# Last stage of a two-layer attention and expert kernel: residual state and its statistics forward in VectorE's chain, attended values ahead of an up block, fourth norm applied by ScalarE

## The chip, the cores and the metric

One core of one Trainium2 chip runs the whole program. Its engines work side by side and meet through semaphores: TensorE (PE in the rows; PEld is its loading of weights), VectorE (DVE), ScalarE (ACT), GpSimd (POOL), and SyncE (SP), which issues plain DMAs. Each engine does its own instructions strictly in order. The metric is device time in microseconds (us) for one launch, lower is better; what is told is the median over repeated runs.

## What is computed

The input x has 32 batches of 256 tokens by 256 features. Four blocks follow each other, each added to x with a gate tanh(g): an attention on a context of 120 tokens, a feed-forward with 8 experts, a second, linear attention, and a second expert block. Only the last two concern the change. Cut to what matters:

```python
# block 3: linear attention, per batch
Q = heads(norm(x2) @ Wq.T + bq); K = heads(ctx @ Wk.T + bk); V = heads(ctx @ Wv.T + bv)
context  = einsum('ld,le->de', softmax(K, over tokens), V)     # per head
attended = Q @ context
x3 = x2 + tanh(g_xattn[1]) * (attended @ Wo.T + bo)
# block 4: experts, h = norm(x3)
scores = sigmoid(h @ Wr); two best of 8; cw = their normalised weights
mlp = sum over 4 experts: cw[e] * ((silu(h @ Wg[e]) * (h @ Wu[e])) @ Wd[e])
out = x3 + tanh(g_ffn[1]) * (mlp + cw[4]*h + cw[6]*h + cw[7]*relu(h) + causal_conv4(h))
```

## The kernel before

The last stage is the function `finish`. It goes over the batches in a software pipeline: `all_steps` calls `step(s, p)` for s from 2 to 36, and inside one step each engine works on several batches at once. Batch s - 2 gets its linear attention, batch s - 3 its fourth norm, routing and first half of gates and ups, batch s - 4 the rest of its experts, batch s - 5 its output; the combination of block 2 and the third norm's statistics for batch s are in VectorE's list as well. The order of every engine's instructions is written out by hand in five functions called `step`, one for each engine. A wait holds up all that stands behind it on the same engine.

The pieces to know, with their lines in the kernel before:

- TensorE: `turn_c` (L2393) turns the context and writes `bank_c`; it waits until VectorE has read the bank in `x3_new`. Then come `down(s-5, 1)` (L2405), which waits for `hidden_low(., 1)`, `values`, `add_rest`, `turn3`, `keys`, an up block, `turn4` (L2445), `queries` (into `bank_x`, waits for `x_turned`), `turn_k`, a gate block, `context`, `logits`, an up block (L80 into `f_ups`), `attended` (into `bank_x`), `output` (into `bank_c`), `down(s-4, 0)` and a gate block.
- VectorE: `own_heads` (L2249, `f_cx`) takes `context` and feeds `attended`. `hidden` (L2158, called twice) makes the product of gates and ups. `route_and_combine` is a chain of small routing instructions in which the two `combine_first` (L1730), the two `combine_second` (L1735), the statistics of the third norm, `hidden_low` (L2212) and `x3_new` (L2330, `f_x`) fill the gaps. After the chain (its last member is L2322) come `weights_turned` (L2143), `stat4` (L2163, L2168), a `silu`, `values_out`, `normalise4` (L2188, `f_x4h`) and `close`.
- ScalarE: `hidden_high` (L2039) follows `hidden`; `x3_own` (L2087, `f_x3p`) follows in its order; `x_turned` (L2045, `f_xT`) empties the turned x3 for `queries`; `attended_out` (L2099) empties `attended` for `output`; `tanh` is L2026.
- GpSimd: `shares` (L1972 to L1978) waits for the whole routing chain; then `keep_x2` (L1947), `norm4` (L1956 to L1961: variance, minus mean, power -1/2, gated share), four gathers by indirect DMA (L1695), `norm3`, and `add_relu` (L1984), which waits for `x3_own`.
- SyncE: `spread_weights` writes the turned weights to DRAM with four DMAs (L1916), waits for them, and reads them back spread over all partitions (L1919, `f_cw_wide`); VectorE's `share_ups` (L2150) wants them in the middle of the next step, before `own_heads`.

## Time and profile before

| | |
|---|---|
| median of 3 runs | 2277.44 us (2277.32 to 2280.03) |
| profiled execution | 2278.87 us, span 2277.1 us |
| granted TensorE clock over the span | 0.993 |
| PE busy | 2174.0 us (95%) |
| DVE busy | 1773.2 us (78%) |
| ACT busy | 1270.6 us (56%) |
| POOL busy | 663.1 us (29%) |

Busy times are sums over the whole span and say which engine has most to do, not which one sets the end of a stage. The last stage begins at 1600 us and takes the remaining 677 us; one of its steps takes a little over 20 us. Times in the rows further down are microseconds from the start of the span; the second number is how long the instruction (or the merged group) ran.

### The profile page before, as it was taken

To read this page: it belongs to the slowest core of one execution; us is meant where nothing else is said; L and a number is where in the kernel's file an instruction comes from. 1 tells how busy PE (TensorE), PEld (TensorE's weight loads), DVE (VectorE), ACT (ScalarE), POOL (GpSimd) and SP (SyncE) were. 2 spreads that over 40 slices of the span, in tenths; PEclk is the share of its full clock that TensorE was granted. 3 is DMA by queue.
4 is the path that set the end of the run, shared out by engine and by line. 5 is a ranking of instruction groups with operands and counts; after the bars stand their busy time and mean duration, and the time that the engine had idled before them with its cause. 6 is when DMAs were issued, how large, how long until landed. Compare 5 with 4: busy or idle time off the path is not lost. (4 is left out here: it accounts for less than half of the span.)

```text
span 2277.1 us, 49508 instructions
## 1 busy us (share of the span) xinstructions
PE 2174.0 (95%) x15998; PEld 1876.2 (82%) x15998; DVE 1773.2 (78%) x6017; ACT 1270.6 (56%) x3251; POOL 663.1 (29%) x1162
## 2 busy tenths in 40 slices
PE   8999999999999999999899999999888889888897
PEld 6777777777777777777799999999688888888886
DVE  5888888888888888888655555555688898888987
ACT  6776677677677667766343333433344444444443
POOL 1123223222322322322200000001555555555541
PEclk9999999999999999999899999999999999999999
DMA  5321011011011011100322222212232222222221
GB/s 185 120 94 30 29 38 39 20 38 39 22 36 38 23 36 38 36 17 28 102 92 84 84 79 80 84 47 71 68 91 86 73 83 91 91 85 73 86 70 47
DMA packets 118302, 146.55 MB, mean 64 GB/s; under 512 B 17458, under 2 KB 100649, under 8 KB 117920
## 3 DMA queue, kind: packets, MB, share of 16 engines
q1 hardware_dynamic: 104905, 121.98, 17.1%
q0 software_dynamic: 12288, 21.21, 3.3%
q8 instruction: 132, 2.16, 0.4%
q14 instruction: 122, 1.00, 0.2%
q10 hardware_dynamic: 855, 0.19, 0.0%
HBM read 101.04 MB, written 54.66 MB: 68 GB/s over the span
## 5 line engine op out<-in xcount | busy, mean ns | idle before, releaser
L711 ACT ACTIVATE a_prob<-a_prob,a_nmax 128x376 f32<-128x376 f32 x512 | 309.8, 606 | 155.5 <-DVE a_nmax L857 155.4
L1457 ACT ACTIVATE e_hidden<-e_first,keep_b 128x256 f32<-128x256 f32 x320 | 134.1, 471 | 283.3 <-PE e_first L80 282.8
L857 DVE CUSTOM_DVE_ANT_0 a_prob<-a_score,a_mask_row 128x376 f32<-128x376 f32 x512 | 266.7, 540 | 10.8 <-issue 5.6
L80 PE MATMUL e_second<-e_w,e_hidden 128*128 128x256 f32 x1920 | 239.5, 284 | 0.0
L80 PEld LDWEIGHTS e_second<-e_w,e_hidden 128*128 128x128 f32 x1920 | 232.6, 192 | 0.0
L869 DVE TENSOR_SCALAR a_prob<-a_prob,a_rden 128x376 f32<-128x376 f32 x512 | 222.8, 456 | 2.5
L1151 PE MATMUL a_turned<-keep_ident,a_prob 128*128 128x128 f32 (+1 forms) x1536 | 217.7, 278 | 2.8 <-DVE a_probT L876 1.6
L1151 PEld LDWEIGHTS a_turned<-keep_ident,a_prob 128*128 128x128 f32 (+1 forms) x1536 | 173.7, 142 | 43.4 <-issue 27.6
L1142 PE MATMUL a_score<-a_kT,a_qT 64*128 64x376 f32 x1024 | 196.4, 502 | 0.0
L876 DVE COPY a_probT<-a_turned 128x384 f32<-128x384 f32 x256 | 139.8, 546 | 54.7 <-PE a_turned L1151 54.7
L719 ACT ACTIVATE a_probT<-a_turned 128x384 f32<-128x384 f32 x256 | 124.9, 488 | 92.0 <-PE a_turned L1151 91.7
L177 POOL TENSOR_SCALAR r_var<-r_mv 128x2 f32<-128x2 f32 x64 | 12.2, 190 | 562.8 <-issue 501.1
L201 POOL DMA_INDIRECT slots<-r_x2h,r_sidx x128 | 133.7, 1045 | 77.1 <-DVE keep_row L332 46.6
L80 PE MATMUL a_work<-a_wkv,a_kvin 128*128 128x512 f32 (+1 forms) x576 | 154.3, 403 | 1.4 <-DVE a_att L881 1.4
L1695 POOL DMA_INDIRECT w_in<-answers,o_row x128 | 136.6, 1067 | 58.7 <-issue 30.7
L1178 PE MATMUL a_work<-a_probT,a_vo 128*64 128x256 f32 (+1 forms) x1152 | 148.4, 393 | 1.8 <-ACT r_rT L217 1.1
L1504 DVE CAST e_hidden<-e_hidden 128x512 fp32r<-128x512 f32 x160 | 68.5, 428 | 96.7 <-ACT e_hidden L1457 96.5
L1178 PEld LDWEIGHTS a_work<-a_probT,a_vo 128*64 128x64 f32 (+1 forms) x1152 | 75.4, 138 | 81.0 <-issue 50.2
L1690 POOL COPY o_row<-keep_row 128x4 uint32<-128x4 uint32 x32 | 10.1, 314 | 412.3 <-DMA answers<-e_y 412.3
L1142 PEld LDWEIGHTS a_score<-a_kT,a_qT 64*128 64x128 f32 x1024 | 88.1, 186 | 50.3 <-issue 18.4
L2405 PE MATMUL f_total<-f_wd,f_hid 128*128 128x256 f32 x768 | 111.5, 295 | 8.6 <-DVE f_hid L2212 8.6
L80 PE MATMUL e_first<-e_rowsT,keep_w 128*128 128x256 f32 x960 | 118.8, 282 | 0.0
(238 smaller groups left out, 5256.9 us busy)
## 6 DMA issues: line engine op xcount, KB each, us to landing
w_in<-W SPq DMA_DIRECT2D x32, 512.0 KB, 4.2
f_cw_wide<-chosen SPq DMA_DIRECT2D x32, 512.0 KB, 4.1
slots<-a_zeros SPq DMA_DIRECT2D x8, 1280.0 KB, 8.9
keep_rows<-slots SPq DMA_DIRECT2D x40, 256.0 KB, 4.1
answers<-e_y SPq DMA_DIRECT2D x40, 256.0 KB, 2.2
a_xn<-x SPq DMA_DIRECT2D x32, 256.0 KB, 2.9
a_xr<-x SPq DMA_DIRECT2D x32, 256.0 KB, 3.8
x<-r_x SPq DMA_DIRECT2D x32, 256.0 KB, 4.1
```

What stands on the lines that cost most here:

```text
L80: last = nc.tensor.matmul(out, stationary(a, t), moving(b, t), start=start and n == 0, stop=stop and n == len(todo) - 1)
L201: nc.gpsimd.indirect_dma_start(out=t["slots"], out_offset=bass.IndirectOffsetOnAxis(ap=sidx[:, p, n:n + 1], axis=0), in_=x2h[:, p, n // 2] ...
L711: nc.scalar.activation(prob[:, u % 4, a], prob[:, u % 4, a], ACT.Exp, bias=nmax[:, u % 4, a:a + 1], scale=-1.0, accum_out=den[:, u % 4, a: ...
L719: nc.scalar.activation(probT[:, u // 2 % 2, a, :, u % 2 * P:(u % 2 + 1) * P], turned_keys[a], ACT.Copy) \
L857: nc.vector.tensor_tensor_reduce(prob[:, u % 4, a], score[SCORE_AT[u][a]][:, 0:NKV], mask_row[:, p], -1.0, 3.0e38, ALU.add, ALU.min, nmax[ ...
L869: nc.vector.tensor_scalar(prob[:, u % 4, a], prob[:, u % 4, a], rden[:, u % 4, a:a + 1], None, ALU.mult) \
L876: nc.vector.tensor_copy(probT[:, u // 2 % 2, a, :, u % 2 * P:(u % 2 + 1) * P], turned_keys[a]) \
L1142: nc.tensor.matmul(score[SCORE_AT[u][a]][:, 0:NKV], qT[rows, p, m, i * P:(i + 1) * P], kT[rows, p, m], start=True, stop=True).then_inc(sco ...
L1151: last = nc.tensor.transpose(turned_keys[a][0:hi - lo, j], prob[:, u % 4, a, lo:hi], ident[:])
L1178: last = nc.tensor.matmul(out[64 * a:64 * a + 64, 0:S], vo[0:hi - lo, p, j, m, a], probT[0:hi - lo, m % 2, a, j], start=j == 0, stop=j == 2)
L1457: nc.scalar.activation(hidden[:, 2 * j + i], first[:, j, i * CH:(i + 1) * CH], ACT.Relu, bias=b1[:, 2 * j + i, bass.ds(e, 1)]).then_inc(re ...
L1695: nc.gpsimd.indirect_dma_start(out=picked[p][:, n], out_offset=None, in_=t["answers"][0:rows], in_offset=bass.IndirectOffsetOnAxis(ap=row[ ...
```

## The change

Five places are moved or rewritten, and what is computed stays the same.

1. In VectorE's chain `x3_new` goes from behind the sum of the weights to behind the two `max`, ahead of the second `combine_second`. `stat4` is cut in two, `stat4_rows` and `stat4_sum`, and both go into the chain too.
2. `normalise4` is taken from VectorE (subtract and multiply) and given to ScalarE (multiply and add a shift). The shift `sh4` is a new product on GpSimd, and ScalarE does the work between `first_tap` and `x_turned`.
3. On GpSimd `norm4` goes ahead of `keep_x2`.
4. ScalarE's `tanh(s-4, 1)` goes to the head of the step.
5. On TensorE `attended` goes ahead of the up block, which now stands between it and `output`.

```diff
@@ GpSimd, norm4
-                eng.wait_ge(rs4_ok, b + 1)
+                eng.wait_ge(rs4_ok, 2 * b + 1)
+                nc.gpsimd.tensor_tensor(sh4[:], nm4[:], rs4[:], ALU.mult).then_inc(rs4_ok, 1)
                 nc.gpsimd.tensor_tensor(rg4[:], rs4[:], keep["gate"][:, 3:4].to_broadcast([P, QT]), ALU.mult) \
                     .then_inc(rg4_ok, 1)
@@ GpSimd, step
-                if live(s - 2):
-                    keep_x2(s - 2, p)
                 if live(s - 3):
                     norm4(s - 3)
+                if live(s - 2):
+                    keep_x2(s - 2, p)
@@ ScalarE
+            def normalise4(b, p):
+                eng.wait_ge(rs4_ok, 2 * (b + 1))
+                at_least(eng, x4r_ok, QT * (b - 1))
+                at_least(eng, x4_made, b - 1)
+                for i in range(QT):
+                    nc.scalar.activation(x4h[:, p, i], x3[:, p, i], ACT.Identity, scale=rs4[:, i:i + 1],
+                                         bias=sh4[:, i:i + 1]).then_inc(x4h_ok, 1)
@@ ScalarE, step
+                if live(s - 4):
+                    tanh(s - 4, 1)
                 if live(s - 2):
                     context_turned(s - 2)
                     normalise3(s - 2, p)
...
                 if live(s - 4):
-                    tanh(s - 4, 1)
                     first_tap(s - 4, p)
+                if live(s - 3):
+                    normalise4(s - 3, q)
                 if live(s - 2):
                     x_turned(s - 2)
@@ VectorE, route_and_combine
                 for i in range(QT):
                     chain(nc.vector.max(top[:, i], sel[:, i]))
+                if live(b + 1):
+                    x3_new(b + 1, 1 - p)
                 if combining:
                     early["combine_second"](eng, c, cp, 1)
...
                 chain(nc.vector.reduce_sum(cws[:], cw[p], AX.X))
                 if live(b + 1):
-                    x3_new(b + 1, 1 - p)
+                    stat4_rows(b + 1, 1 - p)
                 wait_chain()
                 chain(nc.vector.tensor_scalar(cws[:], cws[:], 1e-9, None, ALU.add))
+                if live(b + 1):
+                    stat4_sum(b + 1)
@@ VectorE, step
-                if live(s - 3):
-                    stat4(s - 3, q)
...
-                if live(s - 3):
-                    normalise4(s - 3, q)
@@ VectorE, relu
+                eng.wait_ge(x4h_ok, QT * (b + 1))
                 eng.wait_ge(own_ok, N_OWN * b + 2)
@@ TensorE, step
                     logits(s - 3, q)
+                if live(s - 2):
+                    attended(s - 2)
+                if live(s - 3):
                     gate_up(s - 3, 0, 1)
                 if live(s - 2):
-                    attended(s - 2)
                     output(s - 2)
```

How VectorE's instructions stand in the second half of its chain, before (`f_x3` is `x3_new`, `f_hid2` is `hidden_low`, `f_stats4` and `f_mv4` are `stat4`):

```order
L2287 MAX f_top<-f_sel 128x8 x2
L1735 SCALAR_TENSOR_TENSOR w2_in<-w1_in,keep_weight,o_xa 128x256
L2293 MAX_INDEX f_topi<-f_top,f_sel 128x8 x2
...
L2212 SCALAR_TENSOR_TENSOR f_hid2<-f_hid,f_hid2 128x512
L2308 TENSOR_TENSOR f_cwp<-f_cwp,f_rsg 128x2x8
L1752 BN_AGGR o_mv3<-o_stats3 128x2 x2
L2312 TENSOR_REDUCE f_cws<-f_cwp 128x2
L2330 SCALAR_TENSOR_TENSOR f_x3<-f_bank_c,keep_gate,f_x2k 128x512
L2316 TENSOR_SCALAR f_cws<-f_cws 128x2
L2318 RECIPROCAL f_cws<-f_cws 128x2
```

And the same place now:

```order
L2295 MAX f_top<-f_sel 128x8 x2
L2342 SCALAR_TENSOR_TENSOR f_x3<-f_bank_c,keep_gate,f_x2k 128x512
L1735 SCALAR_TENSOR_TENSOR w2_in<-w1_in,keep_weight,o_xa 128x256
L2303 MAX_INDEX f_topi<-f_top,f_sel 128x8 x2
...
L2219 SCALAR_TENSOR_TENSOR f_hid2<-f_hid,f_hid2 128x512
L2318 TENSOR_TENSOR f_cwp<-f_cwp,f_rsg 128x2x8
L1752 BN_AGGR o_mv3<-o_stats3 128x2 x2
L2322 TENSOR_REDUCE f_cws<-f_cwp 128x2
L2176 BN_STATS f_stats4<-f_x3 128x6 x2
L2326 TENSOR_SCALAR f_cws<-f_cws 128x2
L2183 BN_AGGR f_mv4<-f_stats4 128x2 x2
L2330 RECIPROCAL f_cws<-f_cws 128x2
```

`x3_new` has moved ahead of ten rows, `hidden_low(., 1)` (`f_hid2`) among them, and the statistics of the fourth norm now stand inside the chain, ahead of its last three members.

GpSimd from the shares to the gathers, before:

```order
L1978 TENSOR_TENSOR f_own<-f_own,f_nm4 128x2
L1947 TENSOR_TENSOR f_x2k<-w2_in,o_bo 128x512
L1956 TENSOR_SCALAR f_var4<-f_mv4 128x2
L1957 TENSOR_SCALAR f_nm4<-f_mv4 128x2
L1959 TENSOR_TENSOR f_rs4<-f_var4,o_minus_half 128x2
L1961 TENSOR_TENSOR f_rg4<-f_rs4,keep_gate 128x2
L1690 COPY o_row1<-keep_row 128x4
```

And now:

```order
L1980 TENSOR_TENSOR f_own<-f_own,f_nm4 128x2
L1957 TENSOR_SCALAR f_var4<-f_mv4 128x2
L1958 TENSOR_SCALAR f_nm4<-f_mv4 128x2
L1960 TENSOR_TENSOR f_rs4<-f_var4,o_minus_half 128x2
L1962 TENSOR_TENSOR f_sh4<-f_nm4,f_rs4 128x2
L1963 TENSOR_TENSOR f_rg4<-f_rs4,keep_gate 128x2
L1948 TENSOR_TENSOR f_x2k<-w2_in,o_bo 128x512
```

The norm still stands behind the shares; it has passed `keep_x2` and gained one product.

ScalarE from the head of a step, before:

```order
L2012 ACTIVATE f_cT<-f_bank_c 128x240
L2019 ACTIVATE f_x3h<-w2_in,o_sh3,o_rs3 128x256 x2
L2026 ACTIVATE f_th<-f_gates1 128x512
L2033 ACTIVATE f_cv<-f_x4p,o_conv_b,o_conv_w 128x256 x2
L2045 ACTIVATE f_xT<-f_bank_x 128x512
L2060 ACTIVATE f_x4T<-keep_bank 128x512
```

And now:

```order
L2036 ACTIVATE f_th<-f_gates1 128x512
L2014 ACTIVATE f_cT<-f_bank_c 128x240
L2021 ACTIVATE f_x3h<-w2_in,o_sh3,o_rs3 128x256 x2
L2043 ACTIVATE f_cv<-f_x4p,o_conv_b,o_conv_w 128x256 x2
L2029 ACTIVATE f_x4h<-f_x3,f_sh4,f_rs4 128x256 x2
L2055 ACTIVATE f_xT<-f_bank_x 128x512
L2070 ACTIVATE f_x4T<-keep_bank 128x512
```

`f_xT`, for which TensorE's `queries` waits, now stands behind the two new `f_x4h`.

## Rows read from the trace of the kernel before

**Rows 1.** Waits, 1651.9 to 2202.34: engine, waiting line, releaser: total, times, longest

```profile
PE f_bank_c L2393 <- DVE f_x L2330: 40.8, 27, 1.8
PE f_bank_c L1886 <- ACT f_aT L2099: 18.6, 27, 0.7
```

**Rows 2.** Timeline: four starts of own_heads (start, duration, engine, line, operands)

```profile
1846.48 0.61 DVE L2249 SCALAR_TENSOR_TENSOR f_cx<-f_bank_c,f_ksum,o_heads 128x128 f32<-128x128 f32 x2 [0.24 <-PE f_bank_c L1886]
1866.80 0.61 DVE L2249 SCALAR_TENSOR_TENSOR f_cx<-f_bank_c,f_ksum,o_heads 128x128 f32<-128x128 f32 x2 [0.24 <-PE f_bank_c L1886]
...
2213.50 0.61 DVE L2249 SCALAR_TENSOR_TENSOR f_cx<-f_bank_c,f_ksum,o_heads 128x128 f32<-128x128 f32 x2 [0.24 <-PE f_bank_c L1886]
2232.36 0.61 DVE L2249 SCALAR_TENSOR_TENSOR f_cx<-f_bank_c,f_ksum,o_heads 128x128 f32<-128x128 f32 x2 [0.24 <-PE f_bank_c L1886]
```

**Rows 3.** Timeline: x3_new, and turn_c behind it

```profile
1855.64 0.75 DVE L2330 SCALAR_TENSOR_TENSOR f_x<-f_bank_c,keep_gate,f_x2k 128x512 f32<-128x512 f32 x1
...
1856.54 0.40 PE L2393 MATMUL f_bank_c<-keep_ident,o_cin 120*128 120x120 f32 x2 [1.48 <-DVE f_x L2330]
```

**Rows 4.** Timeline: second hidden, combines, x3_own, add_relu

```profile
1848.92 0.71 DVE L2158 TENSOR_TENSOR f_hid<-f_hs,f_hid 128x512 f32<-128x512 f32 x1
...
1850.63 1.08 ACT L2087 ACTIVATE f_x3p<-f_x,f_own 128x256 f32<-128x256 f32 x2
1850.84 0.47 DVE L1730 SCALAR_TENSOR_TENSOR o_xa<-w_in,keep_weight 128x256 f32<-128x256 f32 x1
...
1851.39 0.38 DVE L1730 SCALAR_TENSOR_TENSOR o_xa<-w_in,keep_weight 128x256 f32<-128x256 f32 x1
...
1851.79 1.62 POOL L1984 TENSOR_TENSOR f_x3p<-f_x3p,f_x4r 128x512 f32<-128x512 f32 x1 [2.70 <-ACT f_x3p L2087]
...
1852.33 1.36 DVE L1735 SCALAR_TENSOR_TENSOR w_in<-w_in,keep_weight,o_xa 128x256 f32<-128x256 f32 x1
```

**Rows 5.** Timeline of another step: add_relu starts just ahead of combine_second

```profile
1892.51 1.28 POOL L1984 TENSOR_TENSOR f_x3p<-f_x3p,f_x4r 128x512 f32<-128x512 f32 x1 [2.69 <-ACT f_x3p L2087]
1892.52 1.56 DVE L1735 SCALAR_TENSOR_TENSOR w_in<-w_in,keep_weight,o_xa 128x256 f32<-128x256 f32 x1
```

**Rows 6.** Timeline: from the chain's end over the other engines

```profile
1854.73 0.68 DVE L2212 SCALAR_TENSOR_TENSOR f_hid<-f_hid 128x512 fp32r<-128x512 f32 x1
...
1856.67 1.49 PEld L2405 LDWEIGHTS f_total<-f_wd,f_hid 128*128 128x128 f32 x12
...
1856.91 0.16 DVE L2322 TENSOR_TENSOR f_cws<-f_cwp 128x2 f32<-128x2 f32 x1
...
1857.25 0.71 DVE L2163 BATCH_NORM_STATS2 f_stats<-f_x 128x6 f32<-128x256 f32 x2
1857.28 0.19 POOL L1972 TENSOR_TENSOR f_own<-f_cws,f_rg 128x2 f32<-128x2 f32 x1 [3.87 <-DVE f_cws L2322]
...
1858.13 1.28 POOL L1947 TENSOR_TENSOR f_x2k<-w_in,o_bo 128x512 f32<-128x512 f32 x1
...
1859.49 0.19 POOL L1956 TENSOR_SCALAR f_var<-f_mv 128x2 f32<-128x2 f32 x1
...
1860.77 0.74 DVE L2188 TENSOR_SCALAR f_x4h<-f_x,f_mv,f_rs 128x256 f32<-128x256 f32 x2 [0.91 <-POOL f_rs L1959]
1860.77 0.57 ACT L2045 ACTIVATE f_xT<-f_bank_x 128x512 f32<-128x512 f32 x1
...
1860.82 0.19 POOL L1961 TENSOR_TENSOR f_rg<-f_rs,keep_gate 128x2 f32<-128x2 f32 x1
...
1862.68 1.60 PEld L1886 LDWEIGHTS f_bank_x<-f_xT,late 128*128 128x128 f32 x8
```

**Rows 7.** Timeline of SyncE: it issues the read of the spread weights

```profile
1859.53 0.35 SPq L1919 DMA_DIRECT2D f_cw_wide<-chosen  x1
```

**Rows 8.** SyncE's waits, 1700 to 2200: total, times, longest

```profile
SPq L1919 <- DMA chosen<-f_cw_rows: 24.6, 24, 2.3
```

**Rows 9.** DMAs into f_cw_wide: from issue to landing

```profile
DMA to landing us min/median/max: 3.3/4.1/4.7
```

More of the change, by code:

```diff
@@ L1801, in finish @@
         rs4 = sb("f_rs4", [P, QT])
+        sh4 = sb("f_sh4", [P, QT])
         nm4 = sb("f_nm4", [P, QT])
@@ L1989, in step @@
                     shares(s - 4, p)
+                if live(s - 3):
+                    norm4(s - 3)
                 if live(s - 2):
                     keep_x2(s - 2, p)
-                if live(s - 3):
-                    norm4(s - 3)
                 if live(s):
@@ L2158, in hidden, with stat4_rows @@
                 nc.vector.tensor_tensor(hid[:, j], hs[:, j], hid[:, j], ALU.mult).then_inc(hid_ok[j], 1)
-            def stat4(b, p):
+            def stat4_rows(b, p):
                 eng.wait_ge(x3_ok, b + 1)
@@ L2163, in stat4, with stat4_sum @@
                     nc.vector.bn_stats(stats4[:, i], x3[:, p, i]).then_inc(stats4_ok, 1)
+            def stat4_sum(b):
                 eng.wait_ge(stats4_ok, QT * (b + 1))
@@ L2181, in close @@
                                                keep["gate"][:, 3:4], x3p[:], ALU.mult, ALU.add).then_inc(yo_ok, 1)
-            def normalise4(b, p):
-                eng.wait_ge(rs4_ok, b + 1)
-                at_least(eng, x4r_ok, QT * (b - 1))
-                at_least(eng, x4_made, b - 1)
-                for i in range(QT):
-                    nc.vector.tensor_scalar(x4h[:, p, i], x3[:, p, i], mv4[:, i, 0:1], rs4[:, i:i + 1],
-                                            ALU.subtract, ALU.mult).then_inc(x4h_ok, 1)
             def key_max(b):
@@ L2351, in step @@
                     values_out(s - 2)
-                if live(s - 3):
-                    normalise4(s - 3, q)
                 if live(s - 5):
@@ L2381, in step @@
                     x3_new(s - 2, p)
+                    stat4_rows(s - 2, p)
+                    stat4_sum(s - 2)
                 elif live(s - 4):
@@ L2535, in step @@
                     logits(s - 3, q)
+                if live(s - 2):
+                    attended(s - 2)
+                if live(s - 3):
                     gate_up(s - 3, 0, 1)
                 if live(s - 2):
-                    attended(s - 2)
                     output(s - 2)
```

## The prediction

> **What bounds the kernel now.** The busy shares make TensorE look full, but the change touches the last stage alone, so I read that stage: first the waits by line, then one step of the timeline. In the waits, TensorE loses 40.8/27 = 1.51 us a step before `turn_c`, which wants `x3_new`, and 18.6/27 = 0.69 us before `output`, which wants ScalarE's copy of the attended values [rows 1]; VectorE loses 0.91 us before `normalise4` [rows 6]. Look next at `own_heads` (`f_cx`), which starts once a step: 1846.48, 1866.80, so the usual step is 20.32 us. Over the 17 steps from 1866.80 to 2213.50 the mean is 20.39; some steps are longer [rows 2].
>
> The step closes as one loop. From `own_heads` 9.16 us of VectorE's list lead to `x3_new` (1855.64); 0.90 later TensorE starts `turn_c` (1856.54); 10.26 later its own list has brought `context` and the next `own_heads` (1866.80) [rows 2, 3]. 9.16 + 0.90 + 10.26 = 20.32. TensorE's list without its two waits would need 20.32 - 1.51 - 0.69 = 18.1 us. Without them, something else closes the loop; the question is what.
>
> I count all times below from the start of `own_heads`, called 0.
>
> **The change, step by step.** *Attended values forward.* `attended` now starts as soon as `own_heads` is done, and the up block covers ScalarE's copy: the 0.69 wait goes. It also clears ScalarE early. Before, `hidden_high(., 1)` stood behind that copy, and `x3_own` started at 1850.63, or 4.15. Now `hidden_high` can start at the end of the second `hidden`, which starts at 2.44 and lasts 0.71 [rows 4]: about 3.18. `hidden_high` takes some 0.52 from start to the next start (estimate: a ScalarE pass over 512 columns, as `f_xT` 0.57, of which the next overlaps a little [rows 6]), so `x3_own` starts at 3.70 and, at 1.08, ends at 4.78. GpSimd's `add_relu`, 0.08 behind it as before, starts at 4.86.
>
> *What that collides with.* Before, `add_relu` ran from 1851.79, and the `combine_second` of 1852.33 took 1.36, against 0.47 for the `combine_first` of 1850.84, which is alike in shape: 0.89 lost in every step. In another step `add_relu` (alone 1.28) started 0.01 ahead of the other `combine_second`, and that one took 1.56: 1.09 lost [rows 4, 5]. Whoever starts first is served first, and the other waits whole. Now the second `combine_first` starts at 1851.39, or 4.91: 0.05 behind `add_relu`. It is held until 4.86 + 1.28 = 6.14 and ends 0.29 later, as in [rows 5], at 6.43, where alone it would end at 5.29: 1.14 lost, and now ahead of `x3_new`. Were `combine_first` first by a hair, `add_relu` would hold what follows it instead, so this is no matter of luck. The Trainium skill (SBUF — State Buffer, Who interferes with whom) says that a VectorE instruction with two SBUF inputs and a GpSimd instruction that reads SBUF exclude each other for the whole instruction, while one with at most one SBUF input is free. By that rule `x3_new`, with one input in PSUM, would have been the right cover for `add_relu`; the trace agrees on the exclusion (1.36 against 0.47).
>
> *`x3_new` forward.* Its new slot is where the late `combine_second` stood, 5.85, plus 1.14: 6.99. Output is done by then (it starts 0.7 earlier than it did). `turn_c` could start at 7.9 instead of 10.06. This loop would close at 18.1, so it no longer binds.
>
> *What waits instead.* Three others:
>
> (a) Fourth norm. In the old kernel the last member of the chain (L2322) starts at 1856.91, 4.58 behind the `combine_second` slot. In that stretch the 0.89 goes (it is counted above), and `stat4` comes in: 0.86, my estimate: 0.71 for its two statistics (1857.25) and 0.15 for two aggregates, each as small as a member of the chain (0.16), one of which fills a gap. 6.99 + 4.58 - 0.89 + 0.86 = 11.54. GpSimd's shares start 0.37 later (1857.28), 11.91, and take 0.85 to the next start (1858.13) plus 0.12 for the semaphore: `norm4` starts at 12.88. From its variance to the place of `rg4`, where `sh4` now stands, is 1.33 (1859.49 to 1860.82), and `sh4` takes 0.20: 14.41. ScalarE's two passes take 1.08 as `x3_own` does, `x_turned` starts 0.09 before their end and takes 0.57: 14.45 + 0.99 + 0.57 = 16.01. `queries` loads its weights at 16.06, and from there to the next `own_heads` is 4.12 (1862.68 to 1866.80) [rows 2, 4, 6]. The loop closes at **20.18**. So taking `keep_x2` (1.28) out of the way is eaten by waiting for the chain first and by 1.0 us of ScalarE ahead of `x_turned`. VectorE's saved 0.74 for two passes and its saved wait of 0.91 are real, but lie outside this loop.
>
> (b) `hidden_low(., 1)` was at 1854.73, or 8.25. Now 8.25 + 1.14 - 0.89 + 0.67 (`x3_new` ahead of it) = 9.17; done 0.68 later; `down(s-5, 1)` loads 0.12 behind, 9.97, and from its place to the next `own_heads` is 10.13 (1856.67 to 1866.80) [rows 2, 6]: **20.10**.
>
> (c) The spread weights. From the chain's last member to SyncE's issue was 2.62 (1856.91 to 1859.53), landing takes 4.1 [rows 6, 7, 9]: 11.54 + 6.72 = 18.3, then `share_ups` and the reciprocal (0.85, estimate: 0.68 as a pass of the same width at 1854.73, and a small one): 19.1. Usually hidden. But SyncE's wait of 1.0 on average goes to 2.3, and landing to 4.7 [rows 8, 9]: 21.0 at worst. I take 0.10 a step for it.
>
> *Cover that I take as free:* tanh at the head of ScalarE's step (ScalarE idles there), `keep_x2` later (its reader is a step's half away; it now holds two tiny instructions of VectorE that would wait for TensorE anyway), `sh4` itself beyond (a).
>
> **Sum.** 20.18 + 0.10 = 20.28 against the mean of 20.39: -0.11 for 28 steps, -3.1 us. The two drain steps without combines (18.86 from 2213.50 to 2232.36 [rows 2]) have no collision ahead of `x3_new` and can go at TensorE's 18.1: -1.4. Filling and the last batch: nothing. Together -4.5. The profiled execution took 2278.87 us; its sum, 2274.4, stands 1.4 over the median, so for the median 2277.44 - 4.5 = **2273 us**. That is 0.2%, which is about what a measurement of this kernel can tell from no change.
>
> **Rivals.**
> *Clean gain (chance 0.13).* If `add_relu` comes later than I think, at `max` or `x3_new`, the 1.14 is not in front: (a) closes at 19.04, and the late `combine_second` pays some 0.4. 28 x (19.4 - 20.39) - 1.4 = -29: 2248 us. TensorE's 18.1 is the floor. Against it: `x3_own` hangs on nothing but the second `hidden`.
> *More collisions, no change (0.17).* Gathers now start later on GpSimd (behind `keep_x2` and `sh4`, some 1.3 us), so the third norm's products meet the second `hidden` and the first `hidden_low`; one hand-over of GpSimd's 0.2 to 0.35 us in front of `x3_new` gives 20.4 to 20.6: 2276 to 2281 us. No row shows such a meeting of the power.
> *Slower: the spread weights arrive late (0.20).* They are written 1.1 us later in the loop (11.54 against 10.43 for the chain's last member, 1856.91), and `own_heads` stands behind `share_ups`. It decides once landing comes later than 19.3. If the DMAs meet the gathers more often, so that a step costs 20.75: 28 x 0.36 - 1.4 = +9, 2286 us.
>
> **How the numbers follow.** My forecast (steps of 20.1 to 20.4, 2269 to 2277 us) has 0.50. Half of it and the clean case and a little of the rest are faster by over 0.2% (below 2272.9): 0.41. The other half with the collisions: same, 0.33. Late weights and the worst collisions: slower, 0.26. For 8 in 10 the range runs from 2258, part of the way to the clean case, to 2286.
>
> **What would show it.** After: the second `combine_first` near 1.5 us and the late `combine_second` near 0.47; waits for `f_x` before `turn_c` gone, in their place TensorE waiting for `f_xT`, `f_x4h` or `f_hid`; no VectorE wait for `f_rs`. Wrong if `combine_first` stays at 0.4, or if `share_ups` waits for a DMA.

## The result

Over 19 runs each, beside each other on the same chip, the changed kernel takes 2282.81 us (2277.87 to 2288.03) and the kernel before 2277.97 us (2274.4 to 2280.35). The ratio is 1.0021, 95% interval 1.0014 to 1.0029: slower by 0.2%, where the prediction had 0.2% faster. The profiled execution took 2280.5 us, its span is 2278.7 us, the granted clock 0.993. One execution of the changed kernel in a later comparison, at a granted clock of 0.554 over its whole span, took 3546.18 us and is left out of every number below.

Earlier stages are the same code in both, and the last stage begins 4 us apart in these two executions, so I measure the last stage alone: it takes 682.7 us (from GpSimd's first memset in it at 1596.03 to the end), before 677.1 (from 1600.03). I then list the 32 starts of `own_heads`. Where the 5.6 us are:

| stretch | before | after |
|---|---|---|
| stage start to the third `own_heads` (filling) | 43.2 | 45.1 |
| usual step | 20.32 | 20.30 |
| mean of the 27 full steps | 20.37 | 20.48 |
| the step behind the 27, to 2213 (before) and 2215 (after) | 20.32 | 20.78 |
| step 2213 to 2232 (before), 2215 to 2233 (after) | 18.86 | 17.83 |
| last `own_heads` to the end | 44.7 | 45.9 |

The usual step did not become longer. It hardly became shorter, and there are some long steps among the usual ones (21.91, 21.68, 20.97, 20.8).

First the usual step. Timeline of the changed kernel from one `own_heads` to the next (start, duration, engine, line, operands), the answer to [rows 2 to 6]:

```profile
1845.17 0.61 DVE L2257 SCALAR_TENSOR_TENSOR f_cx<-f_bank_c,f_ksum,o_heads 128x128 f32<-128x128 f32 x2 [0.33 <-PE f_bank_c L1887]
...
1848.89 1.08 ACT L2097 ACTIVATE f_x3p<-f_x,f_own 128x256 f32<-128x256 f32 x2
...
1850.05 1.58 POOL L1986 TENSOR_TENSOR f_x3p<-f_x3p,f_x4r 128x512 f32<-128x512 f32 x1 [0.47 <-ACT f_x3p L2097]
1850.08 0.39 DVE L1730 SCALAR_TENSOR_TENSOR o_xa<-w_in,keep_weight 128x256 f32<-128x256 f32 x1
1850.39 1.27 DVE L2289 TENSOR_TENSOR f_sel<-f_rsg,o_rbias 128x16 f32<-128x16 f32 x1
1851.58 0.47 DVE L1735 SCALAR_TENSOR_TENSOR w_in<-w_in,keep_weight,o_xa 128x256 f32<-128x256 f32 x1
...
1852.12 0.73 DVE L2342 SCALAR_TENSOR_TENSOR f_x<-f_bank_c,keep_gate,f_x2k 128x512 f32<-128x512 f32 x1
...
1853.00 0.40 PE L2403 MATMUL f_bank_c<-keep_ident,o_cin 120*128 120x120 f32 x2
...
1855.01 1.70 PE L2415 MATMUL f_total<-f_wd,f_hid 128*128 128x256 f32 x12 [1.62 <-DVE f_hid L2219]
1856.62 0.16 DVE L2334 TENSOR_TENSOR f_cws<-f_cwp 128x2 f32<-128x2 f32 x1
1856.99 0.19 POOL L1974 TENSOR_TENSOR f_own<-f_cws,f_rg 128x2 f32<-128x2 f32 x1 [5.37 <-DVE f_cws L2334]
...
1858.17 0.19 POOL L1957 TENSOR_SCALAR f_var<-f_mv 128x2 f32<-128x2 f32 x1 [0.29 <-POOL f_own L1980]
...
1859.73 1.09 ACT L2029 ACTIVATE f_x4h<-f_x,f_sh,f_rs 128x256 f32<-128x256 f32 x2 [0.25 <-POOL f_sh L1962]
1860.72 0.57 ACT L2055 ACTIVATE f_xT<-f_bank_x 128x512 f32<-128x512 f32 x1
...
1865.47 0.61 DVE L2257 SCALAR_TENSOR_TENSOR f_cx<-f_bank_c,f_ksum,o_heads 128x128 f32<-128x128 f32 x2 [0.34 <-PE f_bank_c L1887]
```

Look at `add_relu` (`f_x3p` on POOL), at 4.88 from `own_heads`. It costs VectorE 1.11 us, but not in the `combine_first` whose record starts 0.03 behind it. That one takes its usual 0.39, and `add_relu` itself takes 1.58 where it takes 1.28 alone, so here it was GpSimd that waited first. What is held is the small `sel` after that (128x16): 1.27 us, where 0.16 is its time alone. In 22 of 28 steps it is `sel`, in the other six a `combine_first` (1.23 to 1.57). `x3_new` follows at 6.95, the chain's last member at 11.45. GpSimd's shares start at 11.82, `norm4` at 13.00, ScalarE's `f_x4h` at 14.56, `x_turned` at 15.55, the next `own_heads` at 20.30.

Now what TensorE and VectorE wait for in the changed kernel, 1660 to 2200 (total, times, longest), the answer to [rows 1]:

```profile
PE f_total L2415 <- DVE f_hid L2219: 40.6, 26, 1.6
DVE f_hid L2163 <- issue: 2.8, 4, 1.7
DVE o_xa L1730 <- issue: 2.0, 3, 1.3
```

The wait of 1.5 us ahead of `turn_c` has become one of 1.6 us ahead of `down(., 1)`. "issue" stands for a wait whose end the profile does not show. The two rows with it have no row of that kind before. `share_ups` (L2163) waits for the spread weights by its code, and `combine_first` (L1730) for a DMA that brings its rows; the experiments below show that both waits are for these transfers. In the step of 21.91 SyncE issues the read of the spread weights at 1902.27, and `share_ups` starts 4.60 later:

```profile
1902.27 0.35 SPq L1920 DMA_DIRECT2D f_cw_wide<-chosen  x1
...
1906.87 0.69 DVE L2163 TENSOR_TENSOR f_hid<-f_ups,f_cw_wide 128x512 f32<-128x512 f32 x1 [1.71 <-issue]
```

The step of 21.68 is the last of the 27. There the last gather stands 1.26 us later behind `own_heads` than before (2.43 in place of 1.17), and `combine_first` waits for it. The rows of the kernel before (its `own_heads` at 2172.49), and of the changed kernel (2172.48):

```profile
2173.66 1.00 POOL L1695 DMA_INDIRECT w_in<-answers,o_row  x1 [0.30 <-issue]
...
2177.01 0.48 DVE L1730 SCALAR_TENSOR_TENSOR o_xa<-w_in,keep_weight 128x256 f32<-128x256 f32 x1
```

```profile
2174.91 1.00 POOL L1695 DMA_INDIRECT w_in<-answers,o_row  x1 [0.30 <-issue]
...
2178.26 1.23 DVE L1730 SCALAR_TENSOR_TENSOR o_xa<-w_in,keep_weight 128x256 f32<-128x256 f32 x1 [1.34 <-issue]
```

### The profile page after: what moved, and what is told of

It is laid out like the page before. It is cut to its first block and busy times, and to the rows that moved or that the text cites. A ratio compares the mean times of both kernels' runs of the same rounds, so it can differ in the third digit from the quotient of the medians.

```text
span 2278.7 us, 49541 instructions
## 1 busy us (share of the span) xinstructions
PE 2184.9 (96%) x15998; PEld 1889.0 (83%) x15998; DVE 1788.0 (78%) x5953; ACT 1306.6 (57%) x3315; POOL 676.1 (30%) x1194
## 5 line engine op out<-in xcount | busy, mean ns | idle before, releaser
L1695 POOL DMA_INDIRECT w_in<-answers,o_row x128 | 143.2, 1119 | 58.7 <-issue 30.7
L2415 PEld LDWEIGHTS f_total<-f_wd,f_hid 128*128 128x128 f32 x768 | 101.0, 196 | 58.1 <-DVE f_hid L2219 56.6
```

The lines of the kernel that those rows point to most:

```text
L1695: nc.gpsimd.indirect_dma_start(out=picked[p][:, n], out_offset=None, in_=t["answers"][0:rows], in_offset=bass.IndirectOffsetOnAxis(ap=row[ ...
L2415: last = nc.tensor.matmul(total[:, i * D:(i + 1) * D], hid2[:, a, e, i * P:(i + 1) * P], wd2[:, c, e], start=j == 0 and i == 0 and n == 0, ...
```

## The experiments

Sixteen runs follow, one of them the changed kernel again, each with its time against the kernel before on the same chip; between kernels I compare these ratios. "Usual" is the step that occurs most, "mean" that of the 27 full steps, both from the starts of `own_heads` in the one profiled execution; in the last two kernels of the table the steps scatter, and "usual" is the short end where most of them crowd. "Falls" are the `down(., 1)` between 1640 and 2230 us that took over 2.0 us where 1.7 is usual.

| kernel | median us | ratio (95%) | usual | mean | falls |
|---|---|---|---|---|---|
| changed, again | 2285.21 | 1.0033 (1.0021 to 1.0045) | 20.30 | 20.65 | 4 |
| attended alone | 2293.35 | 1.0053 (1.0037 to 1.0070) | 20.52 | 20.86 | 5 |
| attended back | 2267.64 | 0.9945 (0.9930 to 0.9960) | 19.46 | 19.81 | 1 |
| add_relu held | 2275.35 | 0.9958 (0.9945 to 0.9971) | 19.93 | 20.22 | 2 |
| x3 back | 2283.99 | 1.0027 (1.0016 to 1.0039) | 20.43 | 20.58 | 1 |
| norm on VectorE | 2285.27 | 1.0025 (1.0016 to 1.0034) | 20.16 | 20.54 | 4 |
| norm longer | 2300.26 | 1.0068 (1.0056 to 1.0081) | 20.73 | 21.16 | 7 |
| norm first | 2282.21 | 0.9995 (0.9985 to 1.0006) | 19.86 | 20.54 | 9 |
| norm first, filled | 2269.47 | 0.9953 (0.9941 to 0.9965) | 19.86 | 20.06 | 0 |
| last weights | 2283.93 | 1.0004 (0.9995 to 1.0013) | 20.32 | 20.53 | 3 |
| last gathers | 2281.87 | 1.0010 (0.9998 to 1.0021) | 20.30 | 20.44 | 4 |
| changed, filled | 2285.12 | 1.0019 (1.0010 to 1.0028) | 20.31 | 20.44 | 0 |
| last and filled | 2279.01 | 0.9998 (0.9989 to 1.0007) | 20.30 | 20.31 | 0 |
| held and norm first | 2263.05 | 0.9927 (0.9910 to 0.9943) | 19.46 | 19.80 | 1 |
| low forward | 2257.96 | 0.9904 (0.9891 to 0.9917) | 19.2 | 19.61 | 0 |
| values first | 2253.59 | 0.9903 (0.9886 to 0.9921) | 19.15 | 19.56 | 1 |

The kernel before has 20.32, 20.37 and no fall.

### The part that moves attended

*Attended back*: the changed kernel with `attended` again behind the up block.

```diff
-                if live(s - 2):
-                    attended(s - 2)
                 if live(s - 3):
                     gate_up(s - 3, 0, 1)
                 if live(s - 2):
+                    attended(s - 2)
                     output(s - 2)
```

> The changed kernel with attended behind the up block again, as before. My theory: output starts later and ScalarE's copy of the attended values stands ahead of hidden_high again, so add_relu starts some 0.4 us later and now meets combine_second(0) and max, mostly under x3_new; x3_new itself is not held by TensorE (output ends 0.6 us later, at 5.6 to 5.8, ahead of its slot at 5.85). So the usual step falls, to 19.8 to 20.1, and the time is 5 to 12 us below the changed kernel. Rival (the 0.69 us that TensorE waits before output is on the path): usual step up to 20.5 to 21, slower than the changed kernel.

*Attended alone*: the kernel before with this one move made, nothing else.

> The kernel before with one part of the change alone: attended ahead of the up block. Theory: this part alone starts add_relu earlier, so that it meets the second combine_first, ahead of x3_new (the collision moves from behind x3_new to the front of it): x3_new would start some 0.5 us or more later than in the kernel before unless output's earlier end helps, which it does not, since x3_new stood in the chain behind the collision anyway. In the kernel before x3_new starts at 9.16 with one combine_second held for 0.89 ahead of it; with the collision 0.25 longer the step is 20.3 to 20.6 and the time 0 to +0.4%: ratio 1.000 to 1.004. Rival: freeing TensorE's wait of 0.69 ahead of output shortens the step: ratio 0.97 to 0.995.

Undone in the changed kernel, the move is worth 0.76% (1.0021 to 0.9945, 17 us), and its usual step of 19.46 is shorter than the 19.8 to 20.1 expected. Made alone, the move costs 0.53%, a little over the 0 to 0.4% expected. In the timeline of attended alone (`own_heads` at 1848.69) the step reads as in the kernel before, with the collision in another place:

```profile
1853.56 1.57 POOL L1984 TENSOR_TENSOR f_x3p<-f_x3p,f_x4r 128x512 f32<-128x512 f32 x1 [2.27 <-ACT f_x3p L2087]
...
1853.90 1.27 DVE L2281 TENSOR_TENSOR f_sel<-f_rsg,o_rbias 128x16 f32<-128x16 f32 x1
...
1858.05 0.75 DVE L2330 SCALAR_TENSOR_TENSOR f_x<-f_bank_c,keep_gate,f_x2k 128x512 f32<-128x512 f32 x1
...
1858.94 0.40 PE L2393 MATMUL f_bank_c<-keep_ident,o_cin 120*128 120x120 f32 x2 [2.50 <-DVE f_x L2330]
```

`add_relu` is 0.44 earlier after `own_heads` than before (4.87; [rows 4] have 5.31), holds `sel` for 1.11 us where it held `combine_second` for 0.89, `x3_new` is 0.20 later (9.36), and the step is 0.20 longer. The 0.69 us that TensorE no longer waits ahead of `output` it waits ahead of `turn_c`: 2.50 in place of 1.48. The longer usual step makes 5.4 us in 27 steps, under half of the 12 us; the mean step is 0.49 longer, and in five steps the granted clock falls behind that longer wait, where it fell in none before (on such falls see below).

Over the whole stage `sel` takes 1.24 to 1.27 us in 26 of 28 steps of attended alone, in 22 of 28 of the changed kernel, and in 3 of 29 with attended back. There (`own_heads` at 1842.59) `add_relu` meets something else:

```profile
1847.90 0.47 DVE L1735 SCALAR_TENSOR_TENSOR w_in<-w_in,keep_weight,o_xa 128x256 f32<-128x256 f32 x1
1847.94 1.58 POOL L1986 TENSOR_TENSOR f_x3p<-f_x3p,f_x4r 128x512 f32<-128x512 f32 x1 [0.95 <-ACT f_x3p L2097]
...
1848.29 0.22 DVE L2295 MAX8 f_top<-f_sel 128x8 f32<-128x8 f32 x2
1848.46 0.75 DVE L2342 SCALAR_TENSOR_TENSOR f_x<-f_bank_c,keep_gate,f_x2k 128x512 f32<-128x512 f32 x1
1849.12 0.68 DVE L1735 SCALAR_TENSOR_TENSOR w_in<-w_in,keep_weight,o_xa 128x256 f32<-128x256 f32 x1
```

It starts at 5.35, behind `sel`; the two `max` and `x3_new` run beside it at their usual length, and the late `combine_second` loses 0.21. The Trainium skill (SBUF — State Buffer, Who interferes with whom) says that a running GpSimd instruction that reads SBUF shuts out a VectorE instruction with two SBUF inputs, but not one with a single SBUF input. The traces agree for both: `sel` was held in the changed kernel (1.27), `x3_new`, with one input in PSUM, was not held here (0.75).

*Add_relu held*: the changed kernel, in which GpSimd waits for the chain's fifth member (the second `max`) ahead of `add_relu`.

```diff
             def add_relu(b):
+                if b + 1 < B:
+                    eng.wait_ge(route, N_ROUTE * (b + 1) + 5)
```

> The changed kernel, and GpSimd's add_relu is held until the two max of the chain are done, so that it runs under x3_new, which has one input in PSUM. My theory: sel and combine_first no longer lose 1.1 us ahead of x3_new, combine_second behind it loses about 0.5; the usual step falls from 20.30 to 19.3 to 19.8, and with the late DMAs the time by 12 to 25 us. Rival (the collision is not on the loop that binds): no change, 2282 us.

`sel` takes 0.16 to 0.17 in all 28 steps. The ratio is 0.9958, that is 0.63% or 14 us below the changed kernel's, with `attended` still forward. So most of the loss is the place of `add_relu`, not the order on TensorE as such. The usual step, 19.93, is just over the 19.3 to 19.8 expected and 0.47 over that of attended back. Held like this, `add_relu` collides with the late `combine_second`, which pays 0.71 us in most steps, where with attended back it pays 0.21:

```profile
1833.82 1.18 DVE L1735 SCALAR_TENSOR_TENSOR w_in<-w_in,keep_weight,o_xa 128x256 f32<-128x256 f32 x1
```

### The norm's loop

*Norm longer*: two products of GpSimd that nobody reads and that wait for each other, ahead of the power in `norm4`.

```diff
                 eng.wait_ge(var4_ok, 2 * (b + 1))
+                for n in range(2):
+                    by_itself(eng, waited)
+                    nc.gpsimd.tensor_scalar(idle4[:, n], mv4[:, :, 0], 1.0, 0.0, ALU.mult, ALU.add)
```

> The changed kernel with two more tiny GpSimd products (about 0.2 to 0.27 us each) in norm4 ahead of the power. My theory (loop over norm4 and ScalarE's x4h and xT into queries binds): usual step 20.30 + 0.5 = 20.8, time up by 12 to 15 us. Rival (hidden_low before down, or the spread weights, bind and norm4 has slack): up by less than 4 us.

*Norm first*: `norm4` ahead of `shares`, with `nm4` and `rg4` in two buffers each, so that the shares of the batch before can still read theirs.

```diff
-                if live(s - 4):
-                    shares(s - 4, p)
                 if live(s - 3):
                     norm4(s - 3)
+                if live(s - 4):
+                    shares(s - 4, p)
```

> The changed kernel with norm4 ahead of shares on GpSimd (minus mean and gated share in two buffers), so that the norm no longer waits for the end of the routing chain. My theory: the loop over the norm closes 1.4 us earlier and the next one, hidden_low before down(s-5, 1), binds at 20.1: usual step 20.10 to 20.15, time 4 to 6 us below the changed kernel. Rival (the norm's loop does not bind): no change.

Longer by 0.43 in the usual step for the one, shorter by 0.44 for the other: the loop over `norm4` closes the changed kernel's step. Norm first also measures the loop over `hidden_low` and `down(., 1)`, which TensorE waits for there: `down` stands at 9.82, the next `own_heads` 10.04 behind it, so it closes at 19.86 and not at the prediction's 20.10. The time of norm first fell by only 0.26%, since nine steps in 27 took 21.4 or more. Eight of these have no late DMA; the ninth (22.23) is the last full step.

*Norm on VectorE* (the subtract and multiply of the kernel before, in its old place behind `values_out`) and *x3 back* (`x3_new` and `stat4` in their old places) undo two other parts of the change:

```diff
@@ norm on VectorE: ScalarE, step
-                if live(s - 3):
-                    normalise4(s - 3, q)
@@ and VectorE, step
                     values_out(s - 2)
+                if live(s - 3):
+                    normalise4(s - 3, q)
@@ x3 back: VectorE, route_and_combine
-                if live(b + 1):
-                    x3_new(b + 1, 1 - p)
...
                 if live(b + 1):
-                    stat4_rows(b + 1, 1 - p)
+                    x3_new(b + 1, 1 - p)
...
-                if live(b + 1):
-                    stat4_sum(b + 1)
```

> The changed kernel with the fourth norm applied by VectorE again. My theory: xT no longer stands behind x4h on ScalarE, but VectorE waits for the norm with close, key_max and conv behind it, and pays 0.74 again. VectorE's x4h would end near 14.9 (14.2 + 0.66), so turn4 and queries go 0.4 us earlier, then key_max and what follows end later: x4_lower near 17.6, share_ups near 19.8, own_heads near 20.5. Usual step 20.4 to 20.7, time 3 to 10 us above the changed kernel. Rival (ScalarE's 1.0 us ahead of xT is what costs): step 20.0 to 20.1, time 5 us below.

> The changed kernel with x3_new and the fourth norm's statistics back in their old places. My theory: turn_c waits for x3_new again and the old loop closes, now with the collision moved to the first half of the chain at 1.1 instead of 0.9: usual step 20.3 to 20.5 by that loop, and the norm starts later, so the loop over ScalarE's x4h is longer too, 20.8 or more: time 2285 to 2298. Rival (the early x3_new is worthless): within 2 us of the changed kernel.

The usual step is 0.14 shorter with the norm on VectorE and 0.13 longer with `x3_new` back, but both times (1.0025, 1.0027) cannot be told from the changed kernel's. So neither part is seen to gain or lose anything in time, though norm on VectorE has the usual step of its rival (20.0 to 20.1 was said, 20.4 to 20.7 expected). The remaining two parts, `norm4` ahead of `keep_x2` and `tanh` at the head of the step, were not undone alone.

### TensorE's new wait and the granted clock

A step of 21.4 in norm first. Stretches of it: window, length, busy time of PE, PEld, DVE, ACT and POOL with the number of instructions, the granted clock as a share of full speed, the share of the DMA engines, GB/s; and below, TensorE's timeline at the start of the second:

```profile
1705.00:1710.60 5.60, 4.03 (x30) 3.55 (x28) 5.60 (x21) 2.49 (x6) 1.57 (x1) 1.00 0.01 1
1710.60:1713.30 2.70, 2.60 (x12) 2.60 (x13) 2.49 (x15) 0.00 (x0) 0.89 (x3) 0.55 0.00 0
```

```profile
1710.70 2.81 PE L2416 MATMUL f_total<-f_wd,f_hid 128*128 128x256 f32 x12 [1.62 <-DVE f_hid L2220]
```

TensorE stood idle for 1.62 us ahead of `down(., 1)`, and right behind that the granted clock is 0.55, that is, near 1.2 GHz where it had 2.4. `down` takes 2.81 in place of 1.70, and the step is 1.6 us longer (21.43 for 19.86).

*Norm first, filled*: six products of 128x128 whose results go nowhere, between `turn_c` and `down(., 1)`.

```diff
                 if live(s - 2):
                     turn_c(s - 2, p)
+                    if live(s - 5):
+                        keep_busy(nc, bank_x[:, 0:P], ident[:], ident[:], 6)
```

> This is the kernel with the norm ahead of the shares, and with six products of 128x128 by TensorE (128 columns of FP32, into a bank that nobody reads then) between turn_c and down(., 1), where TensorE waits 1.62 us for the second hidden_low in each step. Their results go nowhere. Theory: the steps of 21.4 us in that kernel (9 of 27, the others 19.86) are those in which the granted clock falls right behind this idle 1.62 us: down(., 1) takes 2.4 to 2.9 us there instead of 1.70, and the step is 1.5 us longer. With the products in the wait, no down(., 1) over 2.0 us is left, the usual step stays 19.86 or is up to 0.2 longer, steps over 21 are at most 2, and the time is 8 to 13 us below that kernel's: ratio 0.994 to 0.996. Rival: the clock falls for what lies further back, or the slow steps are those of late DMAs, and the falls stay: ratio 0.999 to 1.001.

All nine falls are gone, the mean step goes from 20.54 to 20.06, and the time falls by 0.42% (0.9995 to 0.9953). The products are free in the usual step, where they fill a wait; in the drain step, where nothing is waited for, they cost 1.3 us (19.10, where norm first has 17.77). The wait in the two kernels, norm first and then filled:

```profile
PE f_total L2416 <- DVE f_hid L2220: 42.1, 26, 1.6
```

```profile
PE f_total L2416 <- DVE f_hid L2220: 7.0, 26, 0.3
```

### Falls and late transfers in the changed kernel itself

The first profile of the changed kernel has no such fall in a full step. It was profiled once more:

> The changed kernel as it is, for the comparison on the same chip. Ratio to the kernel before 1.0015 to 1.003. By the theory of the clock, down(., 1) over 2.0 us may show in a usual step of this execution, 1.1 us lost with each, where the first profile had none; by the rival none shows.

Here there are four, three of them in full steps, and the ratio of 1.0033 is a little over the expected one. Stretches ahead of and in one of them (columns as above), and its `down` in the timeline:

```profile
1691.80:1693.40 1.60, 0.07 (x1) 0.00 (x0) 1.60 (x9) 1.50 (x4) 0.00 (x0) 1.00 0.00 0
1693.50:1696.30 2.80, 2.80 (x13) 2.80 (x14) 2.37 (x14) 0.00 (x0) 0.63 (x4) 0.54 0.00 0
```

```profile
1693.49 2.73 PE L2415 MATMUL f_total<-f_wd,f_hid 128*128 128x256 f32 x12 [1.62 <-DVE f_hid L2219]
```

So the number of falls differs between executions of one kernel, and one profile does not tell their share. Four kernels are there to tell the causes apart. *Last weights*: `share_ups` takes the spread weights of the batch before, from a second buffer. *Last gathers*: that, and from the fourth batch on the combination takes the rows gathered for the batch before. All transfers are still made, none of these is waited for in its own step, and what these two kernels compute is not the right output. (The gathers of last gathers wait for the combination of the batch before, in place of the one before that, so that no row is overwritten too early; this line is not shown.) *Changed, filled* and *last and filled*: the six products as above in the changed kernel and in last gathers.

```diff
-                eng.wait_ge(cw_in, 16 * (b + 1))
+                at_least(eng, cw_in, 16 * b)
...
-                                        ups[j][:].rearrange("p (e s) -> p e s", e=2), cw_wide[:, pair(j)],
+                                        ups[j][:].rearrange("p (e s) -> p e s", e=2), cw_wide[(b + 1) % 2][:, pair(j)],
@@ last gathers: combine_ready and the combination, where last is 1 in VectorE's chain
-        eng.wait_ge(picked_in[p], 16 * QT * 2 * (b // 2 + 1))
+        eng.wait_ge(picked_in[(b - last) % 2], 16 * QT * 2 * ((b - last) // 2 + 1))
...
-        nc.vector.scalar_tensor_tensor(xa[:, i], picked[p][:, 2 * i], share(b, 2 * i),
+        nc.vector.scalar_tensor_tensor(xa[:, i], picked[(b - last) % 2][:, 2 * i], share(b, 2 * i),
```

> The changed kernel, but share_ups multiplies by the spread weights of the batch before (two buffers), so it never waits for this batch's DMA; the weights used are the wrong batch's. My theory: the usual step stays at 20.30 us, because the loop over shares, fourth norm, ScalarE and queries sets it, but the steps of 20.8 and 21.9 that came from late spread weights go; the mean of the 27 middle steps falls from 20.48 to about 20.35 and the time by 3 to 4 us against the changed kernel, about level with the kernel before. Rival (the loss sits in the ends of the stage, or late gathers cause it): under 1 us better, so still 4 to 5 us over the kernel before.

> The changed kernel, in which from the fourth batch on share_ups multiplies by the spread weights of the batch before, and the combination takes the rows that were gathered for the batch before. All transfers are made as before, but none of these two is waited for in its own step. The kernel in which only the weights were the last batch's was 0.17% faster than the changed one. Theory: the mean step of 20.48 stands 0.18 over the usual 20.30 because of transfers that come late; without both, no wait of VectorE for a DMA is left, steps over 20.6 are only those in which the granted clock falls, and the time is 3 to 6 us below the changed kernel's: ratio to the kernel before 0.9995 to 1.0008. Rival: the lateness of the transfers is not what separates the two kernels, and the ratio stays at 1.002.

> The changed kernel with the six products that go nowhere between turn_c and down(., 1), as in the kernel with the norm first. Theory: in the profiled execution of the changed kernel the granted clock did not fall in any usual step, but TensorE waits the same 1.62 us there as in the three kernels beside it (norm on VectorE, last weights, last transfers), of which each shows three or four falls at 1.1 us; so other executions of the changed kernel have falls too, and its times spread over 10 us, where those of the kernel before spread over 6. With the wait filled: usual step 20.3, no down(., 1) over 2.0 us in a usual step, 2 to 5 us below the changed kernel on the same chip. Rival: the changed kernel as such has no falls to lose, and the time stays within 1 us of it.

> The changed kernel with the last batch's spread weights and gathered rows (from the fourth batch on) and with the six products in TensorE's wait. Theory: late transfers and falls of the granted clock are all that separates the mean step of the changed kernel from its usual 20.30; with both away the mean of the 27 full steps is 20.30 to 20.35, the time 5 to 8 us below the changed kernel on the same chip, and at or just under the kernel before: ratio to it 0.9985 to 1.000. Rival: a part of the loss lies elsewhere (filling, the last batch, or other executions' long steps of another kind): the gain is under 3 us.

With both away the mean step is 20.31, its usual length, and the time is that of the kernel before: 0.9998, against 1.0033 for the changed kernel in the same comparison. Late transfers are the clear part: 1.0019 to 0.9998 between the two filled kernels. The falls are the unclear one: last gathers to last and filled is 1.0010 to 0.9998, with intervals that overlap, and the changed kernel's median fell by only 0.1 us when filled (2285.21 to 2285.12), though its ratio fell from 1.0033 to 1.0019. To either figure come the 1.3 us that the products cost in the drain step (19.10 for 17.82).

The times of last weights and last gathers cannot be told apart, but their traces can. Without the wait for this batch's weights, `share_ups` waits nowhere, while the last full step keeps its wait for rows (1.28 us) and takes 21.75. Without the wait for this batch's rows too, that step takes 19.93. The wait for rows in the last full step stands in both profiles of the changed kernel (1.34 and 1.40). Waits of over 0.25 us for the weights stand in three and five other full steps, of 0.30 to 1.71.

### Towards a faster kernel

*Held and norm first* has both cures. *Low forward* adds `hidden_low(., 1)` ahead of `x3_new`, *values first* adds `values_out` ahead of `silu(., 1)`.

```diff
+                if low:
+                    hidden_low(b - 1, 1)
                 if live(b + 1):
                     x3_new(b + 1, 1 - p)
...
-                if low:
-                    hidden_low(b - 1, 1)
@@ values first: VectorE, step
+                if live(s - 2):
+                    values_out(s - 2)
                 if live(s - 4):
                     silu(s - 4, 1)
-                if live(s - 2):
-                    values_out(s - 2)
```

> Both edits: add_relu held until the two max are done, and norm4 ahead of shares. My theory: the two effects add, since they cut different pieces of the same list of loops: usual step 18.9 to 19.4, mean 0.2 above it for late DMAs, time 22 to 38 us below the changed kernel. Rival (spread weights then bind, as they hang on the chain's end): step 19.5, time 18 us below.

> The kernel with add_relu held and the norm first, and the second hidden_low taken from its place behind the sum of the one-hot rows to the place ahead of x3_new. Theory: what closes the step of 19.46 there is hidden_low, down(., 1) and TensorE's list behind it, with 1.43 us of idle TensorE ahead of down(., 1). With hidden_low 2.9 us earlier, down(., 1) starts right behind turn_c, and the idle time goes. TensorE's list alone is 18.0; the next loop is that of the spread weights (the chain's last member at 11.05, issue 2.6 behind it, landing 4.1, share_ups and reciprocal 0.85): 18.6. Usual step 18.1 to 18.8, and 18 to 35 us below that kernel: ratio to the kernel before 0.978 to 0.985, and falls of the granted clock in down(., 1) gone. Rival: the x3_new that is 0.6 us later or the DMAs give the gain back: usual step 19.2 or more, ratio 0.990 or more.

> The kernel with hidden_low forward, and values_out taken from behind silu(., 1) to the place ahead of it in VectorE's list. Theory: hidden_low forward ended at 19.2 and not at 18.6, because TensorE now waits 1.3 us ahead of keys for values_out, which stands in VectorE's list behind the chain and a silu of 0.56; with it 0.56 earlier the loop closes at 18.7 (18.6 to 18.9), where the spread weights, which VectorE waits for in 11 of 27 steps already, take their share of the mean: 6 to 14 us below that kernel, ratio to the kernel before 0.984 to 0.988. Rival: the loop runs over VectorE's own list (the chain behind own_heads), in which nothing gets shorter: usual step 19.2 and ratio 0.990.

Held and norm first gave 0.9927, 0.94% or 21 us under the changed kernel. The two effects add, as the theory said (0.37 and 0.44 of the usual step alone, 0.84 together), but time and step (19.46) lie just outside what was expected. Attended back alone has the same usual and mean step (19.46, 19.81) and a ratio, 0.9945, whose interval overlaps; the two cures together were not tried with it. Low forward gave 0.9904, not the 0.978 to 0.985 of the theory but the numbers of its rival: TensorE's wait went on to `keys`, as the waits of that kernel show (first fence). In values first a part of it moved again, to the spread weights, for which VectorE now waits in 24 steps (second fence) where it was 11 in low forward, and nothing was gained. Both are nearly 1% faster than the kernel before.

```profile
PE f_bank_c L1888 <- DVE f_v L2191: 33.3, 26, 1.5
```

```profile
DVE f_hid L2166 <- issue: 20.1, 24, 2.3
PE f_bank_c L1888 <- DVE f_v L2191: 17.6, 25, 0.9
```

## Why the prediction was wrong

**Right: the collision and what follows on VectorE.** *Attended values forward* put `x3_own` at 3.72 (3.70 was said), `add_relu` at 4.88 (4.86), cost 1.11 us ahead of `x3_new` (1.14), put `x3_new` at 6.95 (6.99) and the chain's last member at 11.45 (11.54). In most steps it was `sel` that paid, not `combine_first`. The prediction had named that case only in passing ("would hold what follows it instead"), and that its price is the same is in part luck: `add_relu` first waited 0.30 itself. The wait ahead of `turn_c` went, and TensorE waits for `f_hid` in its place, as said. Both of the prediction's own signs of being wrong are there: `combine_first` stays at 0.39, and `share_ups` waits for a DMA.

**The step that failed first: the term (a), "20.18".** It measured 20.30. The loop is the right one (norm longer and norm first), but a hand-over in it, from GpSimd's shares to `norm4`, was mis-sized. "Take 0.85 to the next start (1858.13) plus 0.12 for the semaphore" was read from the start of `keep_x2`, which waits for nothing of the shares; the variance starts 1.18 behind the first share (1856.99 to 1858.17), with 0.29 idle. That is 0.21 more than the 0.97 taken, less 0.09 by which the chain was early. Of the 0.14 that the usual step was to gain, 0.02 were left. Term (b), "20.10", was too long (19.86 in norm first), which changed nothing, since (a) was the longer one.

**The step that failed second: what was put at nothing or small.** The late weights had "0.10 a step". The changed kernel's mean stands 0.18 over its usual step in one profile and 0.35 in the other, the kernel before's 0.05. Late transfers carry most of what shows in the time, as the two filled kernels say (-0.21%, 4.8 us). They are not only the weights: "Filling and the last batch: nothing" left out the gathered rows, for which the last full step waits 1.34. A wait of TensorE was moved from one place (1.51) to another (1.62) and taken as worth the same; four falls of the granted clock in one execution, none in another, were no term at all. How many us these cost in the median is not settled: the filled kernel is 0.1 (by the medians) to 3.2 us (by the ratios) faster, and carries 1.3 us of its own products.

**Drain and filling.** The drain's -1.4 was nearly right for the step of 17.83 (-1.03), but the step ahead of it is 20.78, and the stretch from the last `own_heads` gives back 1.2: TensorE waits 2.33 us ahead of `turn4` there (1.26 before) and then 1.41 ahead of a gate block (as before), and runs at half the clock up to 2257.6. The 1.2 belongs to this execution: in the second profile of the changed kernel the waits are the same (2.35, 1.42), but the clock is back after 3 us, as in the kernel before, and the stretch takes 44.9, 0.2 more than before. Stretches of the changed kernel, and of the kernel before at the same place:

```profile
2254.00:2257.70 3.70, 3.70 (x22) 3.70 (x21) 3.14 (x18) 0.72 (x2) 1.28 (x1) 0.59 0.00 0
```

```profile
2254.00:2257.70 3.70, 3.70 (x34) 3.70 (x33) 3.14 (x18) 0.62 (x2) 1.43 (x3) 1.00 0.00 0
```

Filling was 1.9 us longer; the sixteen runs have 40.9 to 45.3, so how much of that is the change is not settled.

**The sum.** The last stage came out 5.6 us longer in the profile where -4.5 was said, 10.1 apart. Of these 6.6 are the 28 steps (half of that the hand-over, 28 times 0.12, the other half long steps), 1.9 the filling, 1.6 the drain step and the stretch behind it.

**The rivals.** The late weights, which gave 2286, had the right sign and part of the cause, but no step of 20.75 as a rule. "More collisions", up to 2281, had the gathers later by 1.3, which came (1.26), but no such collision: no `hidden` takes over 0.73 and no `hidden_low` over 0.69 in the changed kernel's steps. The later gathers cost the wait in the last full step. The clean gain was seen as soon as `add_relu` comes behind `sel`: its step of 19.4 is the 19.46 of attended back. So the change holds parts that together are worth -0.55% (attended back, against the kernel before) and one that costs 0.76% on top of them. The prediction had the price of that part, 1.14, but counted TensorE's 0.69 as saved, which was no gain, since TensorE waits further on anyway. It did not ask what the change would be without it.

## What to carry to other kernels

Price every part of a change alone as well as in the sum: freeing a wait on an engine that waits again further on gives nothing, and may start something else earlier, here `add_relu` by 0.44 us, that then stands in the path of the loop. Choose the place of a GpSimd pass by a wait on the chain, rather than leave it to chance, and count what stands behind that place too: `x3_new` ran freely beside `add_relu`, the `combine_second` behind it lost 0.71. Where a change moves an idle stretch of TensorE, look at the stretch behind it in more than one profiled execution, and compare mean steps beside the usual one.

## What the runs showed of the hardware

- A VectorE instruction of 128x16 with two SBUF inputs took 1.27 us in place of 0.16 beside GpSimd's `add_relu`, and 0.16 to 0.17 in every step when `add_relu` was held back. The price of this collision was the rest of the other's time, not a share of one's own.
- Starts 0.03 us apart did not tell who was served first: `add_relu` at 1850.05 took 1.58 in place of 1.28, and the `combine_first` of 1850.08 its usual 0.39.
- The granted clock fell from its upper level behind 1.62 us of idle TensorE in some steps and not in others of the same kernel, to 0.50 to 0.63 as the mean over `down(., 1)`: in 9 of 26 in norm first, in 4 and 0 in two executions of the changed kernel. With the same stretch filled by products that go nowhere there was none in three kernels. Behind the 1.48 us of the kernel before there was none in its one profile; behind the 2.50 us of attended alone there were five.
- The filling products cost nothing in the usual step (20.30 and 20.31, 19.86 and 19.86) and 1.3 us in the one drain step, in which TensorE waits for nothing (17.8 and 19.1 in all three filled kernels).
